# Experts' second bias moved into the bank of the turned sum, short constant products, all instruction lists anew

## The reference, cut to what matters

```
x = x + ga * attn0(layernorm(x) * (1 + ca) + sa)      # scan: S = a*S - a*b*(S k) k' + b*v k'
h = layernorm(x) * (1 + cb) + sb
x = x + gb * (h + sum_e gate[e] * (silu(h @ we1[e] + be1[e]) @ we2[e] + be2[e]))
x = x + ga1 * ssd1(layernorm(x) * (1 + ca1) + sa1)
x = x + gb1 * butterfly_ffn(layernorm(x) * (1 + cb1) + sb1)
```

## Time and profile before

| what | us |
|---|---|
| three runs of the kernel | 491.87, 489.74, 486.61 |
| their median | 489.74 |
| the profiled execution | 488.66 |
| its span, first to last instruction | 486.8 |
| mean granted PE clock | 0.972 of full speed |

### The profile page before, as it was taken

The page is one execution under the profiler, slowest core; times in us unless marked ns, Lnnn a source line. Parts: engine busy times, 40 slices in busy tenths (PEclk is TensorE's granted clock), DMA queues, the critical chain, the costliest instruction groups (busy, mean ns, idle before and its releaser), DMA issues. The chain is left out here.

```text
span 486.8 us, 7163 instructions
## 1 busy us (share of the span) xinstructions
PE 429.1 (88%) x2164; PEld 312.5 (64%) x2164; DVE 346.9 (71%) x897; ACT 362.7 (74%) x629; POOL 162.7 (33%) x231
## 2 busy tenths in 40 slices
PE   4796987869897899999999999999999878999666
PEld 2675845548684776567667666767677556698434
DVE  3565998759899874999999899998325582222872
ACT  4889779587875759699669885869988889555324
POOL 1143840872359751267840272071100002000010
PEclk9789999799999799999999999999999999999899
DMA  7849892036600338000303811000001000000001
GB/s 199 288 127 267 286 309 80 0 85 173 159 2 0 88 99 213 19 0 1 87 1 85 208 39 23 1 1 0 2 0 24 0 1 1 22 1 1 0 1 23
DMA packets 34630, 35.49 MB, mean 73 GB/s; under 512 B 12824, under 2 KB 30752, under 8 KB 34336
## 3 DMA queue, kind: packets, MB, share of 16 engines
q1 hardware_dynamic: 34016, 30.57, 23.8%
q10 hardware_dynamic: 576, 4.46, 2.6%
HBM read 13.78 MB, written 1.05 MB: 30 GB/s over the span
## 5 line engine op out<-in xcount | busy, mean ns | idle before, releaser
L877 PEld LDWEIGHTS psS<-we2s,hid 128*128 128x128 f32 x1024 | 130.9, 195 | 36.6 <-issue 31.8
L862 PE MATMUL psF<-h,we1s 128*128 128x256 f32 (+1 forms) x384 | 136.8, 465 | 5.6 <-ACT hid L1645 4.8
L877 PE MATMUL psS<-we2s,hid 128*128 128x128 f32 x1024 | 133.4, 279 | 7.4 <-DVE acc L2319 6.6
L1645 ACT ACTIVATE hid<-psF,col 128x256 f32<-128x256 f32 (+1 forms) x192 | 99.6, 542 | 48.8 <-PE psF L862 44.4
L862 PEld LDWEIGHTS psF<-h,we1s 128*128 128x128 f32 x384 | 67.1, 195 | 38.4 <-issue 19.5
L3338 POOL TENSOR_TENSOR QS<-H,qn 128x256 f32<-128x256 f32 x64 | 55.1, 867 | 102.8 <-DVE H L2305 85.2
L2319 DVE SCALAR_TENSOR_TENSOR acc<-psS,gate,acc 128x128 f32<-128x128 f32 x128 | 41.0, 342 | 35.8 <-PE psS L877 35.7
L2305 DVE TENSOR_TENSOR_SCAN H<-A,psT 128x320 f32<-128x320 f32 x64 | 52.2, 816 | 1.3
L1447 ACT ACT_TABLE_LOAD x38 | 48.8, 1283 | 2.3 <-PEq L3646 1.7
L2277 DVE TENSOR_TENSOR psT<-wrep,H 128x360 f32<-128x360 f32 x63 | 40.2, 638 | 14.0 <-DMA wrep<-XX 12.5
L3389 POOL TENSOR_TENSOR x<-x,gdb 128x512 f32<-128x512 f32 (+1 forms) x5 | 4.6, 925 | 130.8 <-PE psM L691 129.4
(11 more groups left out here) (267 smaller groups left out, 650.1 us busy)
## 6 DMA issues: line engine op xcount, KB each, us to landing
wrep<-XX SPq DMA_DIRECT2D x72, 160.0 KB, 3.4
krep<-kn SPq DMA_DIRECT2D x64, 128.0 KB, 2.5
hid<-fold_mats_dram SPq DMA_DIRECT2D x22, 256.0 KB, 4.6
we1s<-we_dram ACTq DMA_DIRECT2D x1, 2048.0 KB, 10.8
we2s<-we_dram ACTq DMA_DIRECT2D x1, 2048.0 KB, 17.2
outT_dram<-x SPq DMA_DIRECT2D x3, 256.0 KB, 3.3
x<-xT_dram SPq DMA_DIRECT2D x2, 256.0 KB, 7.5
worep<-wo_rep_dram SPq DMA_DIRECT2D x1, 512.0 KB
```

What stands on the lines that cost most here:

```text
L862: mm(bank[name][:, 0:(b - a) * TWS[w]], we1s[:, e, k * P:(k + 1) * P], h2[w % 2][:, a * TWS[w]:b * TWS[w]], start=True, stop=True).then_in ...
L877: last = mm(bank[name][:, t * P:(t + 1) * P], hid[n % 2][:, k, t * P:(t + 1) * P], we2s[:, e, k, :], start=(k == 0), stop=(k == HT - 1))
L1645: nc.scalar.activation(hid[x_ % 2][:, k, 0:c], psF[n % 2][:, 0:c], ACT.Silu, bias=pc("be1", HT * e + k)).then_inc(s_hid_done, 1)
```

## The change

It takes `router_bias` off PE and ACT, adds the bias product in `experts_back`, makes expert 0's mix a scaling, gives `gateT` a tile of its own, and lets `fill` go to any bank with 512 or 256 columns. ACT's `gate_rows` of a window now waits until the previous window is turned back.

```diff
-        gateT = br[0:EXPERTS, :].rearrange("p (t n) -> p t n", t=TTM)
+        gateT = sb("gateT", EXPERTS, TTM, P)
...
-            def router_bias(w):
...
             def experts_back(u):
 
+                w = EU[u][0]
+                pe.wait_ge(s_gT_read, w + 1)
                 pe.wait_ge(s_acc_done, mixed(u + 1))
...
-                    last = nc.tensor.transpose(bank[name][:, j * P:(j + 1) * P], acc[EU[u][0] % 2][:, t, :], cst("ident"))
+                    mm(bank[name][:, j * P:(j + 1) * P], acc[w % 2][:, t, :], cst("ident"), start=True, stop=False)
+                    last = mm(bank[name][:, j * P:(j + 1) * P], be2s[:, :], gateT[:, t, :], start=False, stop=True)
...
             def fill(i):
 
-                free(f"F{i % 2}")
-                mm(psF[i % 2][:, :], cst("ident"), C[:, :, :].rearrange("p a n -> p (a n)"), start=True, stop=True)
+                name = list(bank)[i % len(bank)]
+                parts = (4, 2)[i // len(bank) % 2]
+                free(name)
+                mm(bank[name][:, 0:parts * P], cst("ident"), C[:, 0:parts, :].rearrange("p a n -> p (a n)"), start=True, stop=True)
...
                 if i == 0 and w > 0:
-                    act.wait_ge(s_acc0_mm, w)
+                    act.wait_ge(s_lg_mm, w)
...
             def gate_rows(w):
                 t = tiles(w)
                 act.wait_ge(s_gT_mm, w + 1)
-                act.wait_ge(s_lg_mm, w + 1)
+                if w > 0:
+                    act.wait_ge(s_yT_mm, passes(w))
...
                 if e == 0:
-                    dve.wait_ge(s_acc0_done, w + 1)
+                    if w > 1:
+                        dve.wait_ge(s_yT_mm, passes(w - 1))
                     dve.wait_ge(s_gate_done, w + 1)
-                else:
-                    dve.wait_ge(s_acc_done, mixed(u, e - 1) + t + 1)
+                    dve.wait_ge(s_eo_mm, n + 1)
+                    v_.tensor_scalar(acc[w % 2][:, at, :], psS[n % 2][:, t * P:(t + 1) * P], gate[w % 2][:, at, 0:1], None,
+                                     ALU.mult).then_inc(s_acc_done, 1)
+                    return
+                dve.wait_ge(s_acc_done, mixed(u, e - 1) + t + 1)
```

More of the change, by code:

```diff
@@ L1021, in _ @@
             project(3, 0)
-            for i in range(1, 4):
-                first(0, 3, i)
+            first(0, 3, 2)
+            first(0, 3, 3)
+            first(0, 4, 0)
             key_products(2, 0)
+            first(0, 4, 1)
+            first(0, 4, 2)
             key_products(2, 1)
-            first(0, 4, 0)
-            first(0, 4, 1)
             project(3, 1)
@@ L1284, in _ @@
             variance(("ffn", 1))
+            second(3, 6, 1)
             first(3, 7, 3)
-            second(3, 6, 1)
+            logits(4)
             second(3, 6, 2)
-            logits(4)
             second(3, 6, 3)
-            second(3, 7, 0)
-            second(3, 7, 1)
-            first(4, 0, 0)
-            second(3, 7, 2)
+            for i in range(0, 3):
+                second(3, 7, i)
             for i in range(0, 4):
@@ L1296, in _ @@
             second(3, 7, 3)
+            first(4, 0, 0)
             ffn_down(1)
-            first(4, 0, 1)
-            first(4, 0, 2)
-            gate_rows(4)
-            first(4, 0, 3)
+            for i in range(1, 4):
+                first(4, 0, i)
             first(4, 1, 0)
@@ L1325, in _ @@
             first(4, 3, 3)
-            for i in range(0, 4):
-                first(4, 4, i)
+            first(4, 4, 0)
             second(4, 3, 0)
             second(4, 3, 1)
-            for i in range(0, 4):
+            for i in range(1, 4):
+                first(4, 4, i)
+            for i in range(0, 3):
                 first(4, 5, i)
             second(4, 4, 0)
+            first(4, 5, 3)
+            second(4, 4, 1)
             first(4, 6, 0)
-            second(4, 4, 1)
             ssd_out(2)
@@ L1895, in _ @@
             hidden(2, 3, 3)
-            hidden(2, 4, 0)
+            attn_branch(4)
             modulate(("ssd", 0))
-            for i in range(1, 4):
+            for i in range(0, 3):
                 hidden(2, 4, i)
+            ssd_steps(0)
+            hidden(2, 4, 3)
             hidden(2, 5, 0)
+            ssd_in(0)
             hidden(2, 5, 1)
-            ssd_steps(0)
-            attn_branch(4)
             hidden(2, 5, 2)
-            ssd_in(0)
+            ssd_tap(0)
             hidden(2, 5, 3)
-            ssd_tap(0)
             ssd_decay(0)
@@ L1988, in _ @@
             route_exp(4)
-            for i in range(0, 3):
+            for i in range(0, 4):
                 hidden(4, 0, i)
-            gate_rows(4)
-            hidden(4, 0, 3)
             hidden(4, 1, 0)
             hidden(4, 1, 1)
-            router_bias(4)
+            gate_rows(4)
             hidden(4, 1, 2)
@@ L2015, in _ @@
             ssd_shifted(2)
-            hidden(4, 4, 2)
-            hidden(4, 4, 3)
+            for i in range(1, 4):
+                hidden(4, 4, i)
             for i in range(0, 3):
@@ L2045, in _ @@
                 hidden(5, 5, i)
-            for i in range(0, 4):
+            hidden(5, 6, 0)
+            ln_square(("ssd", 3))
+            for i in range(1, 4):
                 hidden(5, 6, i)
-            ln_square(("ssd", 3))
             for i in range(0, 4):
```

1093 lines of the change are left out of this document (533 added, 560 removed).

## The result

The kernel after takes 498.26 us (median of four runs, 497.48 to 500.85) where the kernel before takes 489.12 us (four runs, 486.61 to 491.87). The ratio is 1.0207, with a 95% interval of 1.0167 to 1.0248: 9.1 us slower by the medians (8.2 to 12.1 by the interval), where 5.2 us less was forecast. The profiled execution took 497.87 us, with a span of 496.0 us.

The account below looks back on a forecast made before the run. PE's own work was taken to bound 170 to 377 us, with idle and low clock elsewhere. Stage terms 0 - 3.0 - 3.5 + 1.8 - 0.5 + 0 = -5.2 us took 488.66 to 483.5 us; range 476.5 to 495.0.

Parts of the forecast that it names:

- I take 1.9 us of loss, bounds 1.0 and 2.7: Turnings in experts_back become ordinary fp32 products: 16 more PE records at 0.13 to 0.17 us each, 1.9 us lost.
- operands exchanged: Bias product in the bank of the turned sum: its 32 records stay 32, so 0 change.
- I take 0, with bounds -4 and +6: 0 to 75 us: earlier taps and squares against early expert weights sum to +0.3, taken as 0.
- Rival B: Early weights hold up the head: up to 8 us, 491.5 us; sign: modulation products starting after 21.5 us; chance 0.16.
- 75 to 110: -3.0: 75 to 110 us: waits for a mix and ACT's root go, key products come earlier; -3.0 us, bounds -7.9 and +2.
- the list of signs: Signs of being right: window 2's key products by 106 us, no PE mix wait over 1.5 us between 95 and 170.
- 110 to 170: -3.5: 110 to 170 us: waits of 3.5 and clock of 3.4 us, half taken; -3.5 us, bounds -6.9 and 0.
- rival A: PE's idle in 75 to 170 us follows DVE's chain, waits only change names; 488.0 us, chance 0.17.
- 170 to 377: +1.8: 170 to 377 us, PE's full queue: +1.9 us from the bias change, -0.1 otherwise; +1.8 us.
- Behind 377: -0.5 and 0: 377 to 450 us: earlier mixes, one ACT copy less, -0.5 us; 450 us to the end: 0, bounds -1 and +1.5.
- in the tail the chain is DVE's: After 450 us: DVE sets the chain, so up to 1.7 us of clock from constant products is credited 0.
- D: Bank change does not pay, gate_rows' new wait holds ACT; +3.3 us, 486.8 us; sign: ACT waiting at gate_rows; chance 0.13.

Follow-up runs that it names:

- experiment 3: Kernel after's functions (bias in the bank, products in turn) with the lists and constant products of the kernel before; 495.67 us, ratio 1.0129.
- experiment 6: Kernel after with identity products first and bias products behind them, and load_weights back behind folded(12); 488.30 us, ratio 0.9988.
- experiment 1: Kernel after with all identity products of a pass first and all bias products behind them (grouped); 490.69 us, ratio 1.0044.
- experiment 7: Grouped kernel after without fill(126) and fill(116), the two constant products from 159.7 us; 491.74 us, ratio 1.0055.
- experiment 8: Grouped kernel after without the seven constant products behind 450 us; 494.75 us, ratio 1.0093.
- experiment 9: Grouped kernel after with late weights, and the bias of a pass as one wide product ahead of the identity products; 487.28 us, ratio 0.9962.
- experiment 12: Kernel after with only load_weights back behind folded(12), identity and bias products still in turn; 492.20 us, ratio 1.0069.
- experiment 4: Kernel after's functions with the lists and constant products of the kernel before, identity products first and bias products behind; 490.29 us, ratio 1.0018.
- experiment 10: Grouped kernel after with late weights, and the lists and constant products of the kernel before behind about 377 us; 489.36 us, ratio 0.9999.
- experiment 11: Kernel before with only load_weights moved early, to behind projected(0, 0); 492.89 us, ratio 1.0066.
- experiment 2: Kernel after with experts_back's bias product replaced by one whose weights have 128 rows, still in turn; 489.75 us, ratio 1.0001.
- experiment 5: Grouped kernel after with the lists of the kernel before until about 60 us, late weights included; 489.53 us, ratio 1.0011.

## Why the prediction was wrong

**The step that failed first: "I take 1.9 us of loss, bounds 1.0 and 2.7", in part 1.** It counted 16 more records at 0.13 to 0.17 us each, the price of records in a run of their own kind. The forecast never asked what stands next to what. The change puts 8-row and 128-row weights in turn, and the trace has the price at every border of a pass. It stood in the trace of before too: between the last turning at 299.70 us and the first bias product at 299.90 lie 0.20 us, and to the next 0.21, where records of one kind follow each other after 0.11. Measured: 5.8 us of PE in the trace and 6.3 us on the chip (experiment 3). Grouping takes 3.7 to 3.9 us off the passes and gives back 3.9 us with late weights, 5.4 in the old lists and 7.6 in the new ones, where the clock goes with it. The sign was right, the term was mis-sized by a factor of about three. The price of the 16 records was right as well: with the products grouped the six passes take 9.0 us, 1.9 more than before. What was wrong is the 0 for the bias product's "operands exchanged", which left out where its records would stand. That the pass stands in the one stretch where PE never idles makes it count in full, as the first part of the prediction says of any work there.

**The head: "I take 0, with bounds -4 and +6".** Rival B was the true mechanism, in size by half: not 8 us, but 3.2 to 3.8 in the old lists and 2.4 to 6.1 in the new. Its test was the wrong one. The modulation products started at 19.03 us, not after 21.5, so by the text B was refuted, while the first seed behind the spreading DMA, at 49.23, past the 47 that it also named, had it. The early weights did not delay the first loads that the modulation waits for. They delayed what SP issues behind them, down to two loads of 4 KB, then the ring, and through PE's order the products of the keys. The rule of the Trainium skill ("DMA: Bandwidth & Descriptors", section "Issuing engines are not separate DMA queues") had been weighed and set aside for 1.5 us. The traces agree with it in part: SP's list slipped as the rule has it, while the DMA engines, with a share of 0.98 before and 1.06 after in 16 to 24, did move more with the second issuer, 444 GB/s for 362.

**75 to 110: -3.0, the right sign, but not by the way described.** To see it, I counted the work that PE had done by a given time: its records of each function, priced at that function's median step in the kernel before, without constant products, turning and bias. Against before, the kernel after is 1.1 us of work behind at 75 us and 0.9 ahead at 110, a gain of 2.0. With late weights and grouped products (experiment 6) it goes from 0.4 to 3.7. Experiments 1, 7 and 8, whose lists are the same up to 110 us, gain only 0.5 to 1.2, so one trace does not give this term to better than 1 us. And experiment 3, with the old lists, gains 0.9 here: a part comes from the waits that Part 1 took away, not from the order. The way that was forecast did not come about. The key products of window 2 were to be done by 106 us; the last of them starts at 109.1, and at 108.6 before. The gate came 5 us later (`gate` at 89.11 against 84.26). PE waited 3.6 us for a mix near 100 us, which the list of signs had excluded. The gate had been there for 10 us by then: that scaling stands at 99.75 us behind DVE's chunks. And the constant product of before that the forecast has in 85 to 93 ran at 71.7 us.

```profile
100.22 3.13 PE L866 MATMUL psS<-we2s,hid 128*128 128x128 f32 x16 [3.59 <-DVE acc L2281]
```

**110 to 170: -3.5, a loss in its place.** By the same count the kernel after goes from 0.9 ahead to 1.0 behind, and experiment 6 from 3.7 to 2.2; both have a drop of the clock near the first turning pass (window means of 0.97). Experiments 1 and 9, with 1.00 all through, gain 0.9 each. So even undisturbed the stage gave a quarter of what I took. The waits of the earlier trace rows did not shrink, they changed names:

```profile
143.79 0.46 PE L879 MATMUL psM<-C,acc 128*128 128x128 f32 x2 [1.23 <-issue]
...
162.84 1.13 PE L938 MATMUL psS<-C 128*128 128x512 f32 x2 [1.04 <-DVE acc L2286]
166.58 1.13 PE L851 MATMUL psF<-h,we1s 128*128 128x256 f32 x4 [1.73 <-ACT hid L1622]
```

The turned sum now waits before 143.8 (the row names no releaser, but the last mix of that window starts at 143.34 and takes 0.34), and the constant product for bank S1 at 162.8. That is rival A, for this stage. DVE is busy 53.98 of 60 us, 54.64 before: it sets when mixes are done. The clock part came (1.00 in 158 to 168), and experiment 7 puts what the products give for it at 0.5 to 1.1 us, within the noise.

**170 to 377: +1.8, was far more.** By the count, the kernel after goes from 1.0 to 4.8 us behind. Three passes stand in it, two of 3.2 us, 8.0 us in all against 4.4 for turning and bias before, and one drop of the clock. The second pass also leaves ACT without hidden tiles for 3.29 us:

```profile
375.55 0.47 ACT L1622 ACTIVATE hid<-psF,col 128x256 f32<-128x256 f32 x1 [3.29 <-PE psF L851]
```

**Behind 377: -0.5 and 0.** At the start of the last pass the kernel after is 457.62 - 450.17 = 7.4 us late, 2.6 more than at 377. 1.3 of these are the pass at 431.71 (1.56 us against 0.22); the rest stays open. From there to the end it is 496.0 - 457.62 = 38.4 us against 486.8 - 450.17 = 36.6. The pass takes 1.3 us longer (1.71 us against 0.44), but DVE, which is at a modulation first, reads its result only 0.55 us later, 1.75 us behind the start of the pass instead of 1.20 (before, then after):

```profile
451.37 0.85 DVE L2420 SCALAR_TENSOR_TENSOR x<-psS,mod,x 128x64 f32<-128x64 f32 x4
```

```profile
459.37 0.86 DVE L2387 SCALAR_TENSOR_TENSOR x<-psS,mod,x 128x64 f32<-128x64 f32 x4 [0.50 <-PE psS L880]
```

The rest is about what the low stretch costs that begins at 459.3, behind the pass: experiment 12, with the same pass and none in the tail, takes 37.3 us. I had credited the tail's constant products with nothing, since "in the tail the chain is DVE's", and counted five of the seven. Experiment 8 gives them 3.4 us in the new lists. The order of before reaches its 36.6 us with four such products of its own, and the new one 36.9 with seven. But 36.6 is the best of the five traces with the old tail, which go up to 39.1 (before, 3, 4, 10, 11), while the six with the new tail, its products and no change of rows in turn take 36.9 to 37.5 (1, 2, 5, 6, 7, 9): against two of the old tails (36.6 and 36.8) they gain nothing, against the other three 0.6 to 2.2 us.

**The sum.** By the count of work up to 377 and the times of the last pass and the end, the kernel after loses 1.1 us until 75, gains 2.0 until 110, and loses 1.9 until 170, 3.9 until 377, 2.6 until the last pass and 1.8 behind it, 9.2 us of span in all. The forecast had 0, -3.0, -3.5, +1.8, -0.5 and 0. This says where the time goes, not by which cause: the late head costs more than its 1.1 us (experiment 11), and what it costs appears behind it. Nor do the causes add up: 6.3 us for the bank (experiment 3) and 3.8 for the load (experiment 11) make 10.1 in the old lists, undoing each in the new ones gives 7.6 and 6.1, and undoing both gives 10.0. The chances were off in kind: four rivals stood in the text, and A, B and D all held in part (of D's sign, ACT waited 3.4 us for the turned sum at one `gate_rows`, at 302.28 us), while I priced them as if only one could.

## What to carry to other kernels

Before an operation is folded into another one's loop, look at what then stands in turn on TensorE: products with few rows of weights belong together, ahead of or behind the full ones, not between them. A large load moved early is paid by everything that the other queues issue behind it, small loads included, so its test is the last DMA of the chain in the head, not the first consumer. Gains in stages that several engines share are waits that change names until a trace shows otherwise; work added in the stage where TensorE never idles is paid in full.

## What the runs showed of the hardware

**A change between 128 and 8 rows of weights costs about 0.2 us.** In a run of one kind a record starts 0.11 us after the one before. At a change, the first record of the new kind starts 0.20 us after, and the second 0.21 after the first. The weight loads tell why it may be so. In the kernel after (first fence) the first load of each new kind starts in step with its own product, and with 128 rows throughout (second fence, experiment 2) every load starts one record ahead:

```profile
299.20 0.29 PEld L880 LDWEIGHTS psM<-gateT,be2s 8*128 8x128 f32 x2
299.61 0.30 PEld L879 LDWEIGHTS psM<-C,acc 128*128 128x128 f32 x2
```

```profile
298.53 0.30 PEld L880 LDWEIGHTS psM<-acc,we2s 128*128 128x128 f32 x2
298.75 0.30 PEld L879 LDWEIGHTS psM<-C,acc 128*128 128x128 f32 x2
```

L880's products start at 299.20 in the one and at 298.64, 0.11 us behind their load, in the other. "TensorE: Matmul & The Clock Gate" of the Trainium skill, section "Part 3: Packing small matmuls — row/col tiling", states in its list of what overlaps that a weight load overlaps a running product only where their groups of rows differ. The text above that list in the same section also names a background weight buffer as a way to load ahead. Here the load overlapped where the rows were the same, and did not where 8 rows met 128, so the measurement decides against the list, taken by itself, for whole products like these. Why the load waits at a change is not shown.

**The clock can fall inside a full queue.** PE was busy for all of 294 to 302 us in the kernel after and in experiment 3, and the clock fell at 302.3 and at 302.0. Both times the pass with products in turn was just ending, and in experiment 12 it was the next such pass (368.7 us, with PE busy for 8.57 of the 8.70 us before). Between 170 and 450 us all three traces of kernels with 8-row and 128-row products in turn hold such a drop. Of the nine traces in which they are grouped, or both of 128 rows, one has a drop (experiment 10, behind an idle of 1.09 us), and of the two with the separate bias product (before, experiment 11) none does. That is one trace of each kernel: the products in turn and the drop go together here, and that the few rows are the reason is not shown.

**A small DMA can hold its issuing queue for up to 8.9 us.** The loads of 4 KB at 17.86 and 21.93 us are the example; with late weights (experiment 6) the same two issues took 0.43 and 0.38 us. In all six traces with early weights the two together take 8.9 to 9.3 us of SP, in three of them nearly all of it at the second (8.8 to 8.9 in experiments 2, 7 and 8), and in the eight with late weights 0.8. The load of 4 KB between them takes 0.43 us in all, so the size is not what decides; what the issue waits for is not shown.
